# Copying two adjoining PSUM banks of edge counts in one ScalarE instruction, with a ring of two pairs in place of three single banks

## What is computed

```
msg = x[src] + edge_attr
agg = segment_sum(msg, dst, N)
h   = relu(agg @ W1 + b1) @ W2 + b2
h   = norms over the whole of h, then per feature; h = gelu(h) + x
out = layernorm(x + h)
```

## Time and profile before

| | us |
|---|---|
| three runs | 906.98, 911.76, 913.2 |
| profiled execution | 911.31 |
| its span | 909.3 |
| PE busy | 729.4 |
| DVE busy | 678.4 |
| ACT busy | 383.4 |
| POOL busy | 145.4 |

### The profile page before, as it was taken

How to read it: one execution, slowest core, us unless ns; L and a number is a source line. 1 busy time by engine, 2 the same in 40 slices (tenths; PEclk the granted TensorE clock), 3 DMA queues, 4 the chain that set the end, 5 groups by cost and what they waited for, 6 DMA issues and landing times.

```text
span 909.3 us, 25887 instructions
## 1 busy us (share of the span) xinstructions
PE 729.4 (80%) x9449; PEld 633.5 (70%) x9449; DVE 678.4 (75%) x1185; ACT 383.4 (42%) x841; POOL 145.4 (16%) x91
## 2 busy tenths in 40 slices
PE   3486569888988888988889988889988889989950
PEld 2464448777877777877777877777877777877830
DVE  5844777877878877878877878877878877844576
ACT  0200034355433555433554433554434554424464
POOL 1210022120221220221120221220221220200000
PEclk9987989899999999999999999999999999999975
DMA  6669973443334443334444334443334444303004
GB/s 173 228 216 361 360 262 99 124 147 115 104 100 121 147 144 116 106 97 125 147 144 114 107 94 128 147 144 112 109 93 130 147 144 113 94 25 141 0 1 141
DMA packets 89477, 123.25 MB, mean 136 GB/s; under 512 B 9029, under 2 KB 85018, under 8 KB 89260
## 3 DMA queue, kind: packets, MB, share of 16 engines
q1 hardware_dynamic: 78992, 112.83, 39.9%
q0 software_dynamic: 6240, 5.08, 2.1%
q10 hardware_dynamic: 4228, 5.12, 1.8%
HBM read 118.91 MB, written 4.03 MB: 135 GB/s over the span
## 4 chain that ended last, share of the span: by engine, by line
PE 48%; DVE 26%; issue 11%; DMA 7%; ACT 5%; DVEq 2%; ACTq 1%; POOL 0%; SPq 0%; POOLq 0%
PE bank L693 33%; DVE pool_m L982 12%; DMA edges<-in_edge_attr_dram 5%; PE bank L622 3%; PE bank L672 3%; ACT counts L519 3%; DVE onehot L875 3%; PE bank L740 3%; PE bank L750 2%; PE bank L656 1%; PE bank L636 1%; DMA agg<-in_dst_dram 1%; DMA begins<-listed,tile_slot 1%; DVE node_f L965 1%; DVE node_f L957 1%
## 5 line engine op out<-in xcount | busy, mean ns | idle before, releaser
L519 ACT CAST counts<-bank 128x490 fp32r<-128x490 f32 x625 | 318.3, 606 | 324.0 <-PE bank L672 324.0
L693 PE MATMUL bank<-counts,x_hi 128*128 128x250 f32 x1225 | 293.5, 284 | 29.6 <-ACT counts L519 29.6
L693 PE MATMUL bank<-counts,x_lo 128*128 128x250 f32 x1225 | 290.6, 281 | 0.0
L982 DVE TENSOR_TENSOR pool_m<-listing,turned_lo 128x3328 bf16<-128x3328 bf16 x125 | 236.7, 1893 | 30.1 <-PE bank L672 26.7
L693 PEld LDWEIGHTS bank<-counts,x_hi 128*128 128x128 f32 x1225 | 234.8, 192 | 33.4 <-ACT counts L519 33.4
L672 PE MATMUL bank<-pool_m 128*128 128x98 bf16 x3125 | 211.2, 210 | 33.0 <-ACT counts L519 22.7
L693 PEld LDWEIGHTS bank<-counts,x_lo 128*128 128x128 f32 x1225 | 235.2, 192 | 0.0
L672 PEld LDWEIGHTS bank<-pool_m 128*128 128x128 bf16 x3125 | 161.9, 99 | 77.6 <-ACT counts L519 75.2
L982 DVE TENSOR_TENSOR pool_m<-listing,turned_key 128x2548 bf16<-128x2548 bf16 x125 | 184.5, 1476 | 0.0
L622 PE MATMUL bank<-edges,onehot 128*32 128x128 f32 x3228 | 126.7, 293 | 30.1 <-DMA edges<-in_edge_attr_dram 23.3
L429 POOL DMA_INDIRECT begins<-listed,tile_slot x52 | 101.9, 1959 | 297.1 <-DVE tile_slot L935 265.2
(11 more groups left out here) (149 smaller groups left out, 407.9 us busy)
## 6 DMA issues: line engine op xcount, KB each, us to landing
edges<-in_edge_attr_dram SPq DMA_DIRECT2D x134, 768.0 KB, 4.5
out_dram<-pool_m SPq DMA_DIRECT2D x6, 512.0 KB
begins<-listed,tile_slot POOLq DMA_INDIRECT x52, 4.2
agg<-in_dst_dram SPq DMA_DIRECT2D x1, 768.0 KB
agg<-in_src_dram ACTq DMA_DIRECT2D x1, 768.0 KB
listed<-agg ACTq DMA_DIRECT2D x1, 768.0 KB
begins<-listed,row_slot POOLq DMA_INDIRECT x26, 4.3
w<-in_L_gnn_W_dram ACTq DMA_DIRECT2D x2, 128.0 KB, 2.2
```

Of the source, the lines that this page charges most:

```text
L519: nc.scalar.copy(counts[:, :, k * nodes:(k + 1) * nodes].rearrange("p q (i m) -> p q i m", m=PAIR), cps[k % RING][:, 0:nodes * NT].rearran ...
L693: last = nc.tensor.matmul(sps[:, 0:CHUNK], part[:, q, :], counts[:, q, :], start=(q == 0 and part is x_hi), stop=(q == NT - 1 and part is ...
L982: last = dve.tensor_tensor(to[b % MARKED], values[:, :, 0:n, :].to_broadcast([P, BLOCKS_B, n, INTER]), of.to_broadcast([P, BLOCKS_B, n, IN ...
```

## The change

ScalarE copies banks 2j and 2j+1 in one instruction of 980 elements a partition; bank 24, the odd one, is copied alone. So a chunk has 13 copies in place of 25. The ring is four banks, two pairs: PE may fill a pair when the pair that was last in its banks has been copied. The copy waits until both banks of the pair are filled, and sums and keys are copied after the pair that holds their place: sums after (10, 11) and (22, 23), keys after (20, 21). To make room the accumulators of the edge part move to banks 4 and 5, and one bank of the dense stage from 3 to 5.

```
-RING = 3
+RING = 4
...
-        banks = [psum(f"bank{i}", [P, 512]) for i in range(8)]
+        twins = [psum(f"twin{i}", [P, 2, 512]) for i in range(2)]
+        banks = [twins[i // 2][:, i % 2, :] for i in range(4)] + [psum(f"bank{i}", [P, 512]) for i in range(4, 8)]
         cps = banks[0:RING]
-        eps = [b[:, 0:D] for b in banks[3:5]]
-        turned_sum = [b[:, D:D + SPREAD] for b in banks[3:5]]
+        eps = [b[:, 0:D] for b in banks[4:6]]
+        turned_sum = [b[:, D:D + SPREAD] for b in banks[4:6]]
...
-        hps = [banks[2], banks[3]]
+        hps = [banks[2], banks[5]]
...
-                for k in range(BANKS):
-                    act.wait_ge(banks_done, c * BANKS + (k + 1 + CREDIT))
+                for k in range(0, BANKS, 2):
+                    two = min(2, BANKS - k)
+                    act.wait_ge(banks_done, c * BANKS + (k + two + CREDIT))
                     nodes = BANK * PAIR
-                    nc.scalar.copy(counts[:, :, k * nodes:(k + 1) * nodes].rearrange("p q (i m) -> p q i m", m=PAIR),
-                                   cps[k % RING][:, 0:nodes * NT].rearrange("p (i q m) -> p q i m", q=NT, m=PAIR)
-                                   ).then_inc(banks_free, 1)
-                    if k in SUMS_AT:
-                        j = SUMS_AT.index(k)
-                        copy_sums(c * GPC + (LEAD * GPC + j), j)
-                    if k == KEYS_AT:
-                        copy_keys(c + 1)
+                    to = counts[:, :, k * nodes:(k + two) * nodes].rearrange("p q (a i m) -> p a q i m", a=two, m=PAIR)
+                    of = twins[k // 2 % 2][:, 0:two, 0:nodes * NT].rearrange("p a (i q m) -> p a q i m", q=NT, m=PAIR)
+                    nc.scalar.copy(to, of).then_inc(banks_free, two)
+                    for at in range(k, k + two):
+                        if at in SUMS_AT:
+                            j = SUMS_AT.index(at)
+                            copy_sums(c * GPC + (LEAD * GPC + j), j)
+                        if at == KEYS_AT:
+                            copy_keys(c + 1)
...
                     if k >= RING:
-                        pe.wait_ge(banks_free, c * BANKS + (k + 1 - RING))
+                        pe.wait_ge(banks_free, c * BANKS + (k // 2 * 2 + 2 - RING))
```

## The result

The changed kernel takes 945.05 us (median of four runs, 944.51 to 945.15), the kernel before 910.08 us beside it. The ratio is 1.0383, with a 95% interval from 1.0342 to 1.0424: slower by 3.8%, on the side that was forecast, but more than twice as much as forecast (35.0 us in place of 15.8) and outside the range. The profiled execution took 945.12 us, its span is 943.1 us, 33.8 us more than the span before.

The account below looks back on a forecast made before the run. No engine is full; a chain of waits, 27.3 us a chunk, bounds the kernel. 0 + 0.02 + 0.61 = 0.63 us a chunk, times 25 = 15.8 us, gives 927.5 us; the 8-in-10 range is 919 to 939.

Parts of the forecast that it names:

- Head: Start of a chunk, filling banks 0 to 4 until DVE can start batch 3; forecast cost 0.
- middle: DVE's 10.2 us until PE turns the keys, with PE and ScalarE's ring beside it; forecast cost 0.02 us a chunk.
- tail: From turned keys to summing matmuls: keys, last banks and one sum on ScalarE; forecast 0.61 us a chunk more.
- six signs: Trace checks: 325 copies, PE's waits for counts and keys, ScalarE's last run, DVE's idle time, period 27.9 to 28.0 us.
- The price of a pair: ScalarE's fused copy: 1.014 us long, 0.876 from start to start, against 0.936 for two singles, saving 0.06 us.
- the long cast: Profile row of 6272 elements in 5420 ns, used to price a copy at 0.833 ns an element.
- a tie: At the keys' turn: PE ready at 444.22 against DVE's 444.24; 0.02 us a chunk taken for jitter.
- The walk: Step-by-step timing of the ring of PE and ScalarE, putting bank 20 at 443.10 against 442.06 before.
- rival A: At the turn of the keys, PE, not DVE, sets the time: 0.1 to 0.35 us a chunk more, 931 to 938; chance 0.14.
- rival D: Granted clock: more waiting in chunks may add or remove a low stretch, 3 to 5 us either way; chance 0.05.

Follow-up runs that it names:

- aligned: Changed kernel with bursts after banks 3, 9, 15, 21 and keys turned after bank 21, so neither splits a pair; 907.83 us, ratio 1.0011 to the kernel before.
- after_fill: Changed kernel plus 12 matmuls a chunk that sum nothing of use, on PE ahead of the wait for the last copies; 928.07 us, ratio 1.0223.
- before_fill: Kernel before plus 10 matmuls a chunk that sum nothing of use, filling PE's idle time ahead of the sums; 906.15 us, ratio 0.9961.
- ring4: Kernel before with a ring of four single banks, one copy a bank, accumulators moved as in the change; 907.28 us, ratio 0.9995.
- before_delay: Kernel before with a small extra ScalarE copy of 120 elements, and a wait for its end, ahead of bank 24's copy; 950.54 us, ratio 1.0455.

## Why the prediction was right in its sign and wrong in its size

**The path.** Head, middle and tail were the right pieces, and the cause was the named one: bursts and keys stand between the banks of a pair. aligned shows it, since moving just these brings the whole loss back. Four of the six signs held: 325 copies; PE's wait for keys down to 0.2 us; the last run beginning 0.77 us after the keys are turned (0.71 forecast); DVE's idle time ahead of its add 2.36 us in a chunk without a low stretch (2.4 forecast; the mean over all chunks is 3.0, because the low clock lengthens it). Two missed: PE's wait at the sums rose to 1.6 us and not to 1.9, and the period to 28.14 us and not to 27.9 to 28.0.

**The price of a pair.** 1.014 us long and 0.876 apart was forecast, 1.00 and 0.895 measured. The row of the long cast gave the element price well; the hidden part of the fixed cost is a little smaller for pairs.

**The middle: the mis-sized term of the order.** I forecast a tie and took 0.02 us; it was 0.21. The walk had bank 20 at 11.60 us after the first bank; it came at 11.82. A copy starts 0.50 us after the weight load of a bank that follows a burst (505.94 to 506.44) and 0.60 after one that follows a turn (509.73 to 510.33, 513.58 to 514.18), where I had taken 0.44 and 0.54 from other rows. With pairs 0.02 further apart this adds up over the steps. In a tie each such error lies on the chain in full, and I should have put the middle's case (rival A) higher than 0.14.

**The tail** was forecast at 0.61 us and measured at 0.65.

**The clock: the step that failed.** Order alone would have made 0.82 x 25 = 20.5 us and a time of about 931 us, inside the range; after_fill, the same order with no low stretch, takes 928.07 us, 21.9 us over before_fill. The sum had no term for the clock, and rival D said only that more waiting "may add or remove such a stretch: 3 to 5 us either way". The mechanism was the right one and the size wrong: 9 stretches more, the eleventh counted, 13.6 us more than the loss in the kernel before, and 17 us that filling takes away. I priced one stretch, and did not ask what happens when the same wait grows in all 25 chunks. The earlier trace rows had shown that the clock could fall inside the chunks; how often it would fall, no row of the kernel before could tell. (The low slices of the earlier trace rows are 3, 4, 6 and 8 and the last two, not 4 to 7 as rival D reads them.) The Trainium skill, Perfetto Trace Analysis, Matmul Optimizations, says that the matmul engine scales its power with use, so that matmuls should run back to back; the trace agrees as far as the fills go (17.0, 36 and 9 us gained by work that computes nothing).

**What stays open.** What PE must have done before its clock falls is not settled. In the six kernels with a fill no low stretch is left between 145 us and the last chunk's sums, and 0.29 us more of idle time brought 15 stretches more. But ring4 idles 1.8 us there and has two; before_delay idles 1.6 us there, as the changed kernel does, and loses twice as much. So this idle time is a handle, not the whole cause; something else counts too, perhaps what lies earlier in the chunk, and no run here separates it.

## What to carry to other kernels

When several buffers are released by one instruction, look at what the producer does between filling the first and the last of them: each such piece of work becomes a wait of the consumer, and an item queued behind the pair inherits it. Before merging instructions, see how far apart they start in a row, not how long one is: here 606 ns long copies started 468 ns apart, so two thirds of the fixed cost was hidden and merging was worth 0.04 us a pair, and nothing that could be measured once the order was mended. And when a change lengthens TensorE's waits in a loop, price the clock for every turn of the loop, and try a fill of idle time as a cheap test: it separates order from clock at once.

## What was not expected of the hardware

The granted clock can fall after PE has resumed full work: in the changed kernel 0.6 to 1.4 us after the sums start, at the stretch shown 2.4 GHz from 517.09 for some 0.6 us and then 1.2 GHz for about 3.4 us, at 1.57 us a time. It is no rule of where it falls: in aligned it fell 0.4 us ahead of the sums, while PE stood still. The step is steep: 0.29 us more of idle time a chunk in before_delay raised the clock loss from 5.1 to 37.3 us. And in the changed kernel the low stretches come in a pattern, in every second chunk through most of the run.
